# Rotation table from the reduced angle, and the residual x added in PSUM: a single-core LRU + attention + MoE kernel

## The reference

```python
Lam   = exp(-exp(nu_log)) * (cos(theta) + 1j*sin(theta))     # 64 complex states
Bu    = einsum('blh,nh->bln', u, B_re + 1j*B_im) * gamma
x_t   = Lam * x_(t-1) + Bu_t                                  # scan over 1024 steps
y     = einsum('bln,on->blo', x, Cc).real + einsum('blh,oh->blo', u, D)
x     = x + lru(layernorm(x))
x     = x + ffn(layernorm(x))        # ffn: h = x + attention(rmsnorm(x)); h + moe(rmsnorm(h))
```

## Time and profile before

| what | value |
|---|---|
| median of 3 runs | 997.0 us (996.48 to 999.84) |
| the profiled execution | 999.88 us |
| its span from first to last instruction | 998.1 us |
| PE, DVE, ACT, POOL busy in the span | 872.4, 855.8, 705.4, 389.5 us |
| mean granted TensorE clock | 0.964 |

### The profile page before, as it was taken

One profiled execution on the slowest core, in us unless ns is written; L12 is line 12 of the kernel. 1 busy time (PEld: TensorE's weight loads), 2 busy tenths in 40 slices (PEclk: granted clock), 3 DMA queues, 4 the chain that ended last, 5 costly groups with the idle time before them and its releaser, 6 DMA issues.

```text
span 998.1 us, 18349 instructions
## 1 busy us (share of the span) xinstructions
PE 872.4 (87%) x5978; PEld 362.2 (36%) x5978; DVE 855.8 (86%) x1462; ACT 705.4 (71%) x1511; POOL 389.5 (39%) x615
## 2 busy tenths in 40 slices
PE   0578788999999999999999999999999999889980
PEld 0265531222222222222222222222322246688980
DVE  6988888999999998989989998898799966668662
ACT  1765424888888888888888888888788876545650
POOL 7213340011010054434604535363687403336774
PEclk9798896999999999999999999999999999999995
DMA  7997740011000110101101010010101111122445
GB/s 248 388 393 243 217 125 18 10 33 25 10 25 15 28 25 9 46 11 29 51 10 25 15 43 28 14 47 9 25 31 45 26 39 47 46 60 67 113 150 190
DMA packets 60830, 74.34 MB, mean 74 GB/s; under 512 B 9153, under 2 KB 39105, under 8 KB 60353
## 3 DMA queue, kind: packets, MB, share of 16 engines
q1 hardware_dynamic: 55408, 63.40, 20.9%
q0 software_dynamic: 4608, 9.58, 2.8%
q10 hardware_dynamic: 720, 0.20, 0.1%
HBM read 28.09 MB, written 44.79 MB: 73 GB/s over the span
## 4 chain that ended last, share of the span: by engine, by line
PE 57%; DVE 22%; ACT 9%; issue 6%; POOL 4%; DMA 1%; POOLq 0%; ACTq 0%; DVEq 0%; SPq 0%
PE ps L1690 20%; DVE nmax L1242 12%; PE ps L1680 9%; PE ps L1568 8%; ACT prob L994 7%; PE ps L1789 6%; PE ps L1805 3%; PE ps L1750 2%; PE ps L1587 2%; PE ps L1557 2%; POOL by_token L821 2%; PE ps L1713 1%; POOL by_expert_rows L742 1%; DMA xacc<-x 1%; PE ps L1529 1%
## 5 line engine op out<-in xcount | busy, mean ns | idle before, releaser
L1242 DVE TENSOR_REDUCE nmax<-ps 128x1 f32<-128x1024 f32 x512 | 602.1, 1219 | 42.5 <-PE ps L1568 38.0
L994 ACT ACTIVATE prob<-ps 128x512 f32<-128x512 f32 x1024 | 529.6, 603 | 81.6 <-PE ps L1680 80.0
L1568 PE MATMUL ps<-packs 50*128 50x512 bf16 x1024 | 344.0, 390 | 8.9 <-DVE nmax L1242 5.0
L1680 PE MATMUL ps<-packs 50*128 50x512 bf16 x1024 | 313.6, 385 | 30.4 <-ACT prob L994 20.4
L1690 PE MATMUL ps<-prob,vpad 128*32 128x512 f32 x2048 | 273.8, 607 | 0.0
L1568 PEld LDWEIGHTS ps<-packs 50*128 50x128 bf16 x1024 | 74.6, 94 | 232.3 <-DVE nmax L1242 175.5
L1680 PEld LDWEIGHTS ps<-packs 50*128 50x128 bf16 x1024 | 75.9, 94 | 148.8 <-ACT prob L994 95.5
L553 POOL MEMSET packs<- 2x2048 bf16 x32 | 57.5, 1797 | 172.8 <-PE ps L1680 171.6
L821 POOL DMA_INDIRECT by_token<-wk,vall x80 | 79.8, 997 | 97.5 <-DVE wk L1332 61.0
L1789 PE MATMUL ps<-ws 128*128 128x128 f32 x640 | 87.6, 281 | 3.1 <-DVE ws L1352 2.3
L1789 PEld LDWEIGHTS ps<-ws 128*128 128x128 f32 x640 | 79.0, 194 | 9.0 <-issue 7.2
(11 more groups left out here) (307 smaller groups left out, 880.5 us busy)
## 6 DMA issues: line engine op xcount, KB each, us to landing
by_expert_rows<-prob SPq DMA_DIRECT2D x4, 5016.0 KB, 31.9
packs<-k_parts SPq DMA_DIRECT2D x32, 192.0 KB, 3.4
packs<-q_parts SPq DMA_DIRECT2D x64, 96.0 KB, 2.8
vall<-by_expert_rows SPq DMA_DIRECT2D x80, 66.0 KB
packs<-by_token SPq DMA_DIRECT2D x8, 512.0 KB, 4.6
w<-w_t SPq DMA_DIRECT2D x3, 1024.0 KB, 15.5
q_parts<-front SPq DMA_DIRECT2D x16, 192.0 KB, 3.3
k_parts<-front SPq DMA_DIRECT2D x16, 192.0 KB, 3.4
```

Source lines behind the costliest of these rows:

```text
L994: act.activation(prob[:, v % RING, :], bank(col_bank(pos)), ACT.Exp).then_inc(col_free, 1)
L1242: dve.tensor_reduce(nmax[:, half, par, pair, qt:qt + 1], bank(first, 2), AX_X, ALU.max, negate=True).then_inc(row_free, 1)
L1568: ins = pe.matmul(bank(first + kh), qpack[r:r + ROWS, slot, half, pair, qt * P:(qt + 1) * P], kpack[r:r + ROWS, slot, pair, kh * HALF:(kh ...
L1680: pe.matmul(bank(col_bank(pos)), kpack[r:r + ROWS, slot, head // 2, kt * P:(kt + 1) * P], qpack[r:r + ROWS, slot, half, head // 2, :], sta ...
```

## The change

1. The table: DVE takes the number of turns of t*theta for all 1024 steps (two wide instructions), and the angle that remains, by halves, with the reduced theta in a short and a small part. ACT takes Abs, two Sin, Square and a scaled copy for each half; DVE forms sin = 2*sin(half)*cos(half) twice, with and without sign. The steps come from a POOL iota into x_cos.
2. ACT's list: later_squares comes ahead of save_u(0); the table follows; the two sign changes of wC come behind the table, ahead of norm_u(1).
3. POOL's memsets: the first kpack one moves to the front, the second waits for the turns. The first clears of qpack, and those of vpad, go to ACT in act_batch(1) and act_batch(2).
4. x is added by PE: product_y(b) for b >= 1 begins with eight products of the identity with x in y's banks. ACT copies the sums out (save_sums) in place of DVE's add.
5. The middle parts of batches 0 to 2 are made by ACT instead of POOL.
6. 16 unused products ahead of y(0) instead of 22.

```diff
@@ POOL
+            gp.iota(x_cos, pattern=[[1, L]], base=0, channel_multiplier=0,
+                    allow_small_or_imprecise_dtypes=True).then_inc(steps_in, 1)
+            gp.memset(kpack[0:MAX_PARTS, :, :, :], 1.0).then_inc(pads, 1)
             gp.memset(blank[:, :, 0:H], 0.0).then_inc(zeros, 1)
...
-            for par in range(2):
-                r = par * ODD
-                gp.memset(kpack[r:r + MAX_PARTS, :, :, :], 1.0).then_inc(pads, 1)
-            clear_maxima(0)
-            clear_maxima(1)
+            gp.wait_ge(pads, 2)
+            gp.wait_ge(turns_taken, 1)
+            gp.memset(kpack[ODD:ODD + MAX_PARTS, :, :, :], 1.0).then_inc(pads, 1)
             gp.wait_ge(pads, 3)
-            gp.wait_ge(q_clear, 4)
-            gp.memset(vpad[:, :, :, :, :], 0.0).then_inc(pads, 1)
-            gp.wait_ge(pads, 4)
-            gp.memset(vpad[:, :, :, :, HD:HD + 1], 1.0).then_inc(pads, 1)
...
-                    gp.tensor_copy(parts[:, w, 1, :], rest[:, w, :]).then_inc(mid_ready, 1)
+                    if b == B - 1:
+                        gp.tensor_copy(parts[:, w, 1, :], rest[:, w, :]).then_inc(mid_ready, 1)
@@ ACT
+            def middle_parts(b):
+                for w in range(2):
+                    act.wait_ge(rest_left, 2 * b + w + 3)
+                    act.activation(parts[:, w, 1, :], rest[:, w, :], ACT.Copy).then_inc(mid_ready, 1)
+            def save_sums(b):
+                for half in range(2):
+                    act.wait_ge(y_done, 2 * b + half + 1)
+                    act.activation(xacc[:, b * TILES + half * 4:b * TILES + half * 4 + 4, :]
+                                   .rearrange("p t h -> p (t h)"), bank(6 + half), ACT.Copy).then_inc(sums_saved, 1)
...
                 if not last:
+                    middle_parts(b)
+                    save_sums(b + 1)
                     keep_z(b)
+                if b == 1:
+                    clear_values()
+                if 1 <= b < B - 1:
+                    clear_maxima(b - 1)
                 if b + 3 < B:
                     norm_u(b + 3)
...
+            def table(half):
+                c = slice(half * HALF, (half + 1) * HALF)
+                arcs, sine, cosine = sgn_sin[:, c], x_sin[:, c], bu_back[:, c]
+                act.wait_ge(angle_ready, half + 1)
+                act.activation(arcs, state_back[:, c], ACT.Abs).then_inc(arc, 1)
+                act.activation(sine, state_back[:, c], ACT.Sin, scale=0.5).then_inc(sin_ready, 1)
+                act.wait_ge(arc, half + 1)
+                act.activation(cosine, arcs, ACT.Sin, scale=-0.5, bias=trig[:, 15:16]).then_inc(sin_ready, 1)
+                act.wait_ge(sin_ready, 2 * half + 1)
+                act.activation(cos_t[:, c], sine, ACT.Square).then_inc(sines, 1)
+                act.wait_ge(sines, half + 1)
+                act.activation(cos_t[:, c], cos_t[:, c], ACT.Identity, scale=-2.0, bias=1.0).then_inc(cos_ready, 1)
...
+            def clear_values():
+                act.activation(vpad[:, :, :, :, :].rearrange("p s t h c -> p (s t h c)"),
+                               ones[:, 0:1].to_broadcast([P, 2 * TILES * HQ * VW]), ACT.Copy, scale=0.0).then_inc(padded, 1)
+                act.wait_ge(padded, 1)
+                act.activation(vpad[:, :, :, :, HD:HD + 1].rearrange("p s t h c -> p (s t h) c"),
+                               ones[:, 0:2 * TILES * HQ].unsqueeze(2), ACT.Copy).then_inc(padded, 1)
+            def clear_maxima(slot):
+                for par in range(2):
+                    r = par * ODD
+                    act.activation(qpack[r:r + MAX_PARTS, slot, :, :, :].rearrange("p f a n -> p (f a n)"),
+                                   ones[r:r + MAX_PARTS, 0:1].to_broadcast([MAX_PARTS, 2 * (HQ // 2) * HALF]),
+                                   ACT.Copy, scale=0.0).then_inc(q_clear, 1)
...
+            later_squares()
             save_u(0)
+            table(0)
+            table(1)
+            act.wait_ge(w_in, 16 * 12)
+            act.mul(wC[NS:P, 0, :], wC[NS:P, 0, :], -1.0).then_inc(b_scaled, 1)
+            act.mul(wC[:, 1, :], wC[:, 1, :], -1.0).then_inc(b_scaled, 1)
             norm_u(1)
-            later_squares()
@@ DVE
+            dve.wait_ge(steps_in, 1)
+            step(dve.tensor_scalar(turn, time, turns, ROUND, ALU.mult, ALU.add))
+            step(dve.tensor_scalar(turn, turn, ROUND, None, ALU.subtract))
+            dve.sem_inc(turns_taken, 1)
...
+            for half in range(2):
+                c = slice(half * HALF, (half + 1) * HALF)
+                step(dve.tensor_scalar(angle[:, c], time[:, c], whole, None, ALU.mult))
+                step(dve.scalar_tensor_tensor(angle[:, c], turn[:, c], -TWO_PI[0], angle[:, c], ALU.mult, ALU.add))
+                step(dve.scalar_tensor_tensor(angle[:, c], time[:, c], part, angle[:, c], ALU.mult, ALU.add))
+                step(dve.scalar_tensor_tensor(angle[:, c], turn[:, c], -TWO_PI[1] - TWO_PI[2], angle[:, c],
+                                              ALU.mult, ALU.add))
+                dve.sem_inc(angle_ready, 1)
+            for half in range(2):
+                c = slice(half * HALF, (half + 1) * HALF)
+                dve.wait_ge(sin_ready, 2 * half + 2)
+                dve.scalar_tensor_tensor(sin_t[:, c], x_sin[:, c], 2.0, bu_back[:, c], ALU.mult, ALU.mult)
+                step(dve.scalar_tensor_tensor(sgn_sin[:, c], x_sin[:, c], sign, bu_back[:, c], ALU.mult, ALU.mult))
+            dve.wait_ge(cos_ready, 2)
...
-                    dve.wait_ge(y_done, 2 * b + half + 1)
-                    xb = xacc[:, b * TILES + half * 4:b * TILES + half * 4 + 4, :].rearrange("p t h -> p (t h)")
-                    step(dve.tensor_tensor(xb, bank(6 + half), xb, ALU.add))
+                    if b == 0:
...
+                    else:
+                        dve.wait_ge(sums_saved, 2 * (b - 1) + half + 1)
@@ PE
+                for t in range(TILES if b else 0):
+                    pe.matmul(bank(6, 2)[:, t * P:(t + 1) * P], ident[:, :], xacc[:, b * TILES + t, :],
+                              start=(t % 4 == 0), stop=False, skip_group_check=True)
...
-                pe.wait_ge(y_taken, b + 1)
+                pe.wait_ge(sums_saved, 2 * b)
...
-            unused_products(22, to=6)
+            unused_products(16, to=6)
+            pe.wait_ge(b_scaled, 4)
             product_y(0)
```

More of the change, by code:

```diff
@@ L209, in build_program @@
         act_self = sem("act_self")
-        lam_ready, sin_ready = sem("lam_ready"), sem("sin_ready")
+        lam_ready, sin_ready, cos_ready = sem("lam_ready"), sem("sin_ready"), sem("cos_ready")
+        steps_in, turns_taken, angle_ready, arc = sem("steps_in"), sem("turns_taken"), sem("angle_ready"), sem("arc")
+        sines = sem("sines")
         trig_red = sem("trig_red")
-        y_taken = sem("y_taken")
+        y_taken, sums_saved = sem("y_taken"), sem("sums_saved")
         bu_read, centred, pool_centred = sem("bu_read"), sem("centred"), sem("pool_centred")
@@ L227, in build_program @@
         pads = sem("pads")
+        padded = sem("padded")
         passed = sem("passed")
@@ L629, in _ @@
             gp.wait_ge(v_saved, B)
-            gp.wait_ge(pads, 5)
+            gp.wait_ge(pads, 3)
+            gp.wait_ge(padded, 2)
             fill_values(0, 0)
@@ L851, in _ @@
             act.wait_ge(trig_red, 1)
-            act.activation(trig[:, 3:4], trig[:, 2:3], ACT.Sin, scale=0.5).then_inc(sin_ready, 1)
-            act.activation(trig[:, 5:6], trig[:, 4:5], ACT.Sin, scale=-0.5,
-                           bias=trig[:, 15:16]).then_inc(sin_ready, 1)
-            act.wait_ge(w_in, 16 * 12)
-            act.mul(wC[NS:P, 0, :], wC[NS:P, 0, :], -1.0).then_inc(b_scaled, 1)
-            act.mul(wC[:, 1, :], wC[:, 1, :], -1.0).then_inc(b_scaled, 1)
+            act.activation(trig[:, 7:8], trig[:, 2:3], ACT.Sin, scale=0.5)
             def save_u(b):
@@ L1120, in _ @@
             step(dve.scalar_tensor_tensor(trig[:, 2:3], trig[:, 1:2], -TWO_PI[2], trig[:, 2:3], ALU.mult, ALU.add))
-            dve.scalar_tensor_tensor(trig[:, 4:5], trig[:, 2:3], -1.0, trig[:, 2:3], ALU.mult, ALU.max).then_inc(trig_red, 1)
+            dve.sem_inc(trig_red, 1)
+            whole, part, turns, sign = (trig[:, i:i + 1] for i in (3, 4, 5, 6))
+            dve.memset(sign[0:NS], 2.0)
+            dve.memset(sign[NS:P], -2.0)
+            dve.tensor_scalar(turns, trig[:, 2:3], float(1 / (2 * np.pi)), None, ALU.mult)
+            step(dve.tensor_scalar(whole, trig[:, 2:3], SHORT, None, ALU.add))
+            step(dve.tensor_scalar(whole, whole, SHORT, None, ALU.subtract))
+            step(dve.scalar_tensor_tensor(part, whole, -1.0, trig[:, 2:3], ALU.mult, ALU.add))
+            time, turn, angle = x_cos, bu_back, state_back
+            dve.wait_ge(steps_in, 1)
+            step(dve.tensor_scalar(turn, time, turns, ROUND, ALU.mult, ALU.add))
+            step(dve.tensor_scalar(turn, turn, ROUND, None, ALU.subtract))
+            dve.sem_inc(turns_taken, 1)
```

(31 more changed lines are left out.)

34 lines of the change are left out of this document (7 added, 27 removed).

## The result

The changed kernel takes 1009.5 us (median of 4 runs, 1008.4 to 1011.2), the kernel before beside it 997.9 us (4 runs). The ratio is 1.0112, 95% interval 1.0096 to 1.0129: slower by 11.6 us. Forecast were 1008.5 us and a sum of +11.5. The profiled execution of the changed kernel took 1009.9 us with a span of 1008.2.

A forecast was written before the change was run, and what follows sets the result against it. It took the setup to be one relay with no engine full, held by ACT's queue in batch 0. -10.1 + 6.6 + 1.6 + 3.0 + 2.5 + 7.9 = +11.5 on the median 997.0 gave 1008.5 us, range 995 to 1016.

The forecast's parts named there:

- The start: Setup up to y(0): new table and earlier squares let y(0) end at 44.9 instead of 55.0 us, gain 10.1.
- rival (e): Table on ACT: slower pace or loads of Abs, Sin and copies, gain at y(0) only 5, total 1013.6; chance 0.08.
- four switches of sets: ACT's table: if abs were not in every set, four switches would add 10.6 us; the sum assumed none.
- ACT's queue in batch 0: Middle parts and save_sums(1) ahead of keep_z and norm_u(3) in ACT's queue delay PE's turn_u(3) by 6.6 us.
- rival (c): PE's clock also falls in batch 0, ahead of turn_a(0): +2.9, total 1011.4; chance 0.18.
- The identities: Chain to y(2): PE's eight identity products adding x, 1.8 us, booked as +1.6.
- The clears ahead of norm_a(2): ACT after y(2): clears make norm_a(2) start 9.6 us behind y instead of 6.5, +3.0.
- y(3): Step up to y(3)'s end, booked in the sum as +2.5 us.
- The last half: After y(3): PE waits for save_v, then runs slow products; turn_a(3) 15.1 us behind y(3) instead of 7.2, +7.9.
- Nothing after it hangs on an absolute time: Attention after the setup: no fixed times there, so a shift of the setup's end shifts the program's end.
- Rival (a): ACT has room: its new work falls into idle gaps, leaving -10.1 + 5.4, about 992 us; chance 0.12.
- Rival (d): Start: DVE's second-half tensor_scalar meets POOL's pow; angle, table and norm_u(1) 1.7 us later, total 1010.2; chance 0.06.

The follow-up runs named there:

- e7: Changed kernel with 24 unused products added in PE's wait ahead of turn_a(0); 1008.2 us, ratio 1.0085 against the kernel before.
- e1: Changed kernel with the clears of qpack and vpad taken from ACT and put on POOL; 997.8 us, ratio 0.9991 against the kernel before.
- e4: Kernel before with only the change's new start, clears on POOL behind its roots, adding x and middle parts as before; 997.8 us, ratio 0.9989.
- e6: Changed kernel with the middle parts of batches 0 to 2 back on POOL; 1009.5 us, ratio 1.0107 against the kernel before.
- e3: Changed kernel with keep_z(0) and norm_u(3) put ahead of the middle parts and copies of y(1) in ACT's list; 1009.6 us.
- e2: Changed kernel with the addition of x back on DVE, without identity products or ACT's copies of sums; 1000.8 us, ratio 1.0018 against the kernel before.
- e8: Kernel before with the new start, fourth fill quarter and experts' weights later in SP's queue, unused products in PE's waits ahead of turn_u(1) and turn_a(0); 990.3 us.
- e10: Kernel before, old start, with the fourth fill quarter and the experts' weights moved later in SP's queue; 1005.6 us, ratio 1.0069.

## Why the prediction was right, and where it was not

**The start: -10.1 forecast, -10.04 measured.** The first state multiply (30.1 against 29.96), the end of later_squares (22.3; its successor starts at 22.17) and y(0)'s end (44.9 against 44.97) came as worked out. The 512-wide operations of the table last 0.61 to 0.71 us, where 0.5 was taken, but each starts 0.52 to 0.65 us behind the one before, so that the table, worked out from 23.3 to 28.7, runs from 23.09 to 28.85. It is ahead of norm_u(1) in ACT's list, for which PE's turn of u(1) waits, so a slower pace would have cost its whole length, as rival (e) says. (The 0.92 us between "two 1024-column copies" are in the earlier trace rows those from a copy to the keep_z behind it.) The L1134 step that took 1.29 us beside POOL's memset takes 0.17 now.

```profile
13.95 0.17 DVE L1198 TENSOR_SCALAR rx<-mvx 128x16 f32<-128x16 f32 x1
...
22.00 0.48 DVE L1211 TENSOR_SCALAR wk<-wk,trig 128x512 f32<-128x512 f32 x1
```

```profile
23.09 0.62 ACT L970 ACTIVATE att<-wk 128x512 f32<-128x512 f32 x1
23.61 0.62 ACT L971 ACTIVATE wk<-wk 128x512 f32<-128x512 f32 x1
24.13 0.71 ACT L973 ACTIVATE wk<-att,trig 128x512 f32<-128x512 f32 x1
...
28.22 0.63 ACT L977 ACTIVATE att<-att 128x512 f32<-128x512 f32 x1
```

The Abs (L970) and the Sin (L971) follow each other with no table load between them. The Trainium skill, "ScalarE: Activation LUTs", section "Table sets: the hidden batching unit", says that abs is in every set; the trace agrees. The price that the prediction gives for four switches of sets, 10.6 us, would have been too high here: in the trace before, the one ahead of L852 took 1.3 us, from the end of one activation at 9.71 to the start of the next at 11.02.

**ACT's queue in batch 0: +6.6 forecast, +9.2 measured** (turn_u(3) 0.84 us sooner after a gain of 10.04). Of this 2.5 are the clock: rival (c), to which the prediction gave 0.18, came true, as e7 shows by taking it away. The forecast had the wait ahead of turn_a(0), 2.9 us, and did not draw from it that q and k would run at the lower level, as they do in the trace before behind a wait of 3.02 us in batch 2; that is the term that was missed.

**The identities: +1.6 forecast, +0.6 measured.** (The prediction works out 1.8, and for y(3) 0.9 + 1.8, and books 1.6 and 2.5.) The 16 rows take their 1.8 us. But product_bu(2) takes 4.5 us, not 5.5: the clock came back sooner. The term was right in its kind and 1.0 too large, since I had kept product_bu's price.

**The clears ahead of norm_a(2): +3.0 forecast, +3.0 measured,** with 1.90, 0.31 and 3.82 us as rows and no idle time between them; a clear of 2 partitions costs as much as one of 128. **y(3): +2.5 forecast, +2.64 measured. The last half: +7.9 forecast, +6.7 measured:** the last half, which waits for save_v, began 8.96 us behind y(3), where 8.9 were forecast; what was mis-sized is the score products and the 24 unused ones from a stopped PE, 4.9 us instead of 6.2.

Summed: -10.04 + 9.2 + 0.6 + 3.0 + 2.64 + 6.7 = +12.1 at turn_a(3), and +11.7 at the first reciprocal. The miss of +2.5 in batch 0 and the two terms that were too large cancel but for 0.6 us, so the total is better than its parts.

**What was wrong is what the terms are worth one by one.** "Nothing after it hangs on an absolute time" holds of the attention, of which it was said. In the setup itself one thing does, and none of the prediction's steps has it: batch 0's parts land at 87.0 to 88.9 us in the traces of all eight kernels with the fill in its old place (before, after, e1 to e4, e6 and e7), behind the fill and the weights in SP's queue, though their high parts are made at anything from 55.9 to 66.8 us. By the sum the start is worth 10.1 and the queue of batch 0 costs 6.6. Measured each by itself, the start brings 1.7 us (e4, interval -0.6 to 2.8) and the queue's removal nothing in the median and 1.2 us at the first reciprocal (e3). They fit together only because their sum, -3.5, with the clock's 2.5 and the 1.2 us that product_bu(2) was shorter, moves the high parts of batch 1 from 90.87 to 88.85, about where the DMA would have held them anyway. That the total came out within 0.1 us of the measured 11.6 is in good part luck. Rival (a), with its 992, could not have come out with the fill where it is: e4, in which ACT has neither clears nor adds nor middle parts, is at 997.8. And e1 and e2 don't add up for a reason of the same kind: the high parts of batch 2 wait for batch 1's stores in e1 (112.13) and, with both taken back, in e4 (112.18). That this is the whole of it is not shown.

**Rival (d)** was not decided. DVE's second tensor_scalar (22.00 + 0.48) ended 0.16 us before POOL's pow began at 22.64, and in no run did POOL begin first. Nearest comes e2, where the pow began 0.05 us behind the start of DVE's step, which kept its 0.48 us.

## What to carry to other kernels

When work is made to start sooner, follow the data to the next buffer that must be free and ask for the landing time of the DMA that frees it, and for all that stands ahead of it in the issuing queue; a wait that is zero in the old trace can be the floor of the new one. A bulk transfer that nobody needs yet belongs behind the small stores of the critical path, and has to be moved anew when the schedule shifts. An instruction that waits for the newest result must not stand in an engine's list ahead of work whose inputs are ready, and idle time on an engine is room only if it does not end at the wait that decides.

## What the runs showed of the hardware

- **TensorE's clock.** A wait of 2.96 us ahead of turn_a(0) was followed by about 6 us at a granted clock that fell to 0.50, and 24 products in that wait kept it at 1.00: q and k 6.2 us against 3.7. With turn_u(1) it is the same: 8 transposes take 1.97 us after, behind a wait of 4.57 us, and 1.09 in e8, behind 26 products and a wait of 3.09 us. The length of a wait does not settle it by itself: behind these 3.09 us the granted clock was 1.00 for the next 3.5 us, and behind the 2.96 us it fell.
- **POOL beside DVE.** It is POOL's small steps that stretch here. The same steps (L617, L618) took 0.20 and 0.22 us while DVE stood idle, and 0.64 and 0.60 beside DVE's steps with two inputs. Those took 0.69 and 0.74, as such steps do with POOL idle (0.69 and 0.75 at 19.65 and 20.37):

```profile
26.70 0.20 POOL L617 TENSOR_SCALAR rx<-rx 128x16 f32<-128x16 f32 x1
26.99 0.22 POOL L618 TENSOR_TENSOR rx<-rx 128x16 f32<-128x16 f32 x1
...
27.89 0.64 POOL L617 TENSOR_SCALAR rx<-rx 128x16 f32<-128x16 f32 x1
28.62 0.60 POOL L618 TENSOR_TENSOR rx<-rx 128x16 f32<-128x16 f32 x1
```

```profile
27.78 0.69 DVE L1220 SCALAR_TENSOR_TENSOR att<-wk 128x512 f32<-128x512 f32 x1 [1.55 <-ACT wk L973]
28.39 0.74 DVE L1221 SCALAR_TENSOR_TENSOR att<-wk,trig 128x512 f32<-128x512 f32 x1
```

  The Trainium skill, "SBUF — State Buffer", section "Who interferes with whom", says that a DVE instruction with two SBUF inputs contends with a GpSimd instruction that reads SBUF. The rows of POOL agree.
- **ACT's pace.** A Sin whose bias is a column of a tile takes 0.71 us, one without 0.62. A clear of 2x2048 takes 1.91 us and one of 128x2048 1.90.
- **SP's queue.** Issuing is not free where the DMA engines are full: a group of four small stores takes 1.8 us in SP's queue at its fastest. Behind the fill, in e4, the six groups took 4.2, 1.9, 6.6, 4.8, 3.4 and 1.8 us, and with one fill DMA of 5 MB just ahead the first took 10.1 (e10).
